# Layer 1 of a gated cross-attention kernel: one route for all probabilities, their low part on VectorE, the weights' rounding on ScalarE

## The chip, the cores and the metric

One core of one Trainium2 chip. The metric is the device time of one execution in microseconds (us). The kernel before takes 1699.95 us, the median of three executions (1699.6 to 1700.13).

## The reference, cut to what matters

Two layers run one after the other on x (8 x 128 x 512), each a gated cross-attention and a gated feed-forward block. The change lies in layer 1 and in the feed-forward block behind it:

```python
# layer 1: 32 query heads, 8 key/value heads, head size 128
z  = layernorm(x)
kv = concat([ctx, z], axis=1)               # 256 keys for each batch element
q  = rms_norm(z @ Wq, q_norm_w); k = rms_norm(kv @ Wk, k_norm_w); v = kv @ Wv
p  = softmax(q @ k.T / sqrt(128))           # 4 query heads share a key head
x  = x + tanh(g_xattn[1]) * ((p @ v) @ Wo)
x  = x + tanh(g_ffn[1]) * (layernorm(x) @ W_ffn.T + bias)
```

## The kernel before, in words

Matrix products run in three passes: each fp32 operand is split into a rounded high part (`_hi`) and the rest (`_lo`), and hi·hi, hi·lo and lo·hi are added up. So each operand needs a rounding (a copy) and a subtraction ahead of TensorE.

Layer 1 is cut into 64 items, one for a key/value head t (0 to 7) and a batch element j (0 to 7): `slot1(t, j)` is written once for every engine, and i = 8t + j is its number. A run of eight slots is called a turn below. The counts in the code start at 1, so `exponentials1(i)` works on the item before the one whose scores the slot makes. The slots of all engines are software-pipelined: slot i makes keys and values of item i+2, transposes queries and keys of item i+1, projects the output of item i-2, makes the queries of item i+2, the scores of item i+1 and the attention output of item i-1. Each engine works its list strictly in the written order; semaphores (`wait_ge`) are the only coupling.

The orders in a slot before the change:

- TensorE: `keys_values`, transposes of q, transposes of k, `output_projection1`, `queries`, scores, `attention_output1`.
- ScalarE: `exponentials1`, `qt_hi`, `kt_hi`, `moved_probabilities_hi` (L1246), `kv_out` (L1212, L1213), `q_out` (L1219), `output1_hi` (L1261).
- VectorE: `inverse_sums1` (L1964), `qt_lo` (L2004), `kt_lo` (L2006), `split_lo` (L1912), `accumulate1` (L1968), `probabilities_in_blocks` (L1983), `v_low` (L1922), `k_mean`, `split_hi` (L1906), `k_scaled` (L1929), `q_mean` (L1936), `maxima1` (L1954, with `nb` at L1959), `output1_lo` (L1992).
- GpSimd: `normalised` probabilities (L769), the probabilities' low part (L774), `k_root`, `q_root` (L631).

The probabilities p of an item must be transposed before they meet v. VectorE transposes them in 32 x 32 blocks, SyncE's queue writes the blocks to a DRAM buffer (L594) and, once that has landed, reads them back in the transposed order with four DMAs (L597). ScalarE then rounds them (`pt_hi`) and GpSimd makes the low part (`pt_lo`). The last four items do not take this route: TensorE transposes them into two PSUM banks (`transposed_probabilities1`, L2561), and ScalarE and VectorE split them from there; that also lets their output follow one slot earlier. `lagged(t, j)` says which route a slot takes.

The weights of the next head are loaded in five pieces of 128 x 1024 in a turn. VectorE rounds piece j in slot j (j below 5) and subtracts in slot j+1, so slots 1 to 5 of a turn have a subtraction and slots 0 to 4 a rounding. The last turn has neither.

PSUM has eight banks. The transposes of q and k go into the same banks as the products (`Q1B`, `KVB`), so `queries` waits until VectorE has read the transposed q (`qt_lo`), and banks 4 and 5 (`T0B`, `T1B`) are kept for the last four items.

After the last slot the feed-forward block of layer 1 runs by row tiles b (0 to 7): row statistics on VectorE, a root on GpSimd, `normed_rows` on VectorE, `transpose_rows(3, b)` on TensorE, `transposed_hi`/`transposed_lo`, `last_ffn(b)`, `feed_forward` and the store. Its steps stand between those of the last items, in an order written by hand.

## Time and profile before

| | |
|---|---|
| median of three executions | 1699.95 us |
| the profiled execution's own time | 1700.84 us |
| its span, first to last instruction | 1699.0 us |
| TensorE matmuls busy | 1651.3 us (97%) |
| VectorE busy | 1216.1 us (72%) |
| ScalarE busy | 987.6 us (58%) |
| GpSimd busy | 771.7 us (45%) |
| granted TensorE clock, mean | 0.999 of full speed |

Layer 1's slots fill about 943 to 1671 us of the span. In the 100 us from 1300 on, TensorE is shown busy 97.0%, VectorE 75.6%, ScalarE 58.6% and GpSimd 60.0%. Matmuls are pipelined, and each counts as busy until its modelled end, so that 97% is not TensorE at its peak: how long a slot takes is read better from the starts of one instruction in consecutive slots.

### The profile page before, as it was taken

The page shows a single profiled execution, that of the slowest core. Times are in us where ns is not written, and L with a number is a line of the kernel's source. Part 1 is how long each engine was busy: PE and PEld are TensorE (multiplying, and loading weights), DVE is VectorE, ACT ScalarE, POOL GpSimd, SP SyncE. Part 2 cuts the span into 40 slices and gives each one's busy share as a digit, 9 for nine tenths or more (in the row PEclk, how much of TensorE's full clock was granted, in tenths as well). Part 3 has the DMA queues.
Part 4 walks back from the last instruction along what each step waited for, and adds up shares of the span by engine and source line. Part 5 has one row for each costly group of instructions (what it writes and reads, how often), then busy time and mean ns, then how long its engine had stood idle before and what let it go on. Part 6 is the DMA issues. An engine that isn't in the chain of part 4 may idle for free.

```text
span 1699.0 us, 30580 instructions
## 1 busy us (share of the span) xinstructions
PE 1651.3 (97%) x9789; PEld 1426.0 (84%) x9789; DVE 1216.1 (72%) x2245; ACT 987.6 (58%) x2480; POOL 771.7 (45%) x644
## 2 busy tenths in 40 slices
PE   9999999999999999999999899999999999999998
PEld 8899999999988888888888777787878787777887
DVE  6444437676787777777788877777777777777777
ACT  5344343345767677676776566565656565665663
POOL 2422223211433443534435565566565656665554
PEclk9999999999999999999999999999999999999999
DMA  6444444545233333333332243434343444433311
GB/s 228 170 173 148 148 166 153 192 138 179 78 104 100 117 108 105 111 100 122 102 112 82 80 141 112 154 117 137 122 151 120 134 136 136 133 123 124 128 57 50
DMA packets 123792, 216.24 MB, mean 127 GB/s; under 512 B 11344, under 2 KB 93648, under 8 KB 120144
## 3 DMA queue, kind: packets, MB, share of 16 engines
q1 hardware_dynamic: 123728, 215.43, 38.0%
q8 instruction: 35, 0.57, 0.1%
q14 instruction: 29, 0.24, 0.0%
HBM read 139.89 MB, written 75.50 MB: 127 GB/s over the span
## 4 chain that ended last, share of the span: by engine, by line
PE 44%; DVE 28%; ACT 12%; issue 10%; POOL 4%; DMA 1%; DVEq 0%; SPq 0%; ACTq 0%; POOLq 0%
PE bank L2163 20%; ACT p L1237 7%; PE bank L2340 6%; DVE probabilities_in_blocks L1983 4%; PE bank L2110 4%; DVE v_lo L1922 3%; PE bank L2112 3%; PE bank L2111 3%; POOL k_r L631 3%; DVE nmax L1954 3%; DVE q_ss L1936 2%; PE bank L2298 2%; PE bank L2376 2%; DVE fbias L1929 2%; DVE qt_lo L2004 2%
## 5 line engine op out<-in xcount | busy, mean ns | idle before, releaser
L712 POOL TENSOR_TENSOR pr<-pr,rn 128x512 f32<-128x512 f32 x64 | 67.5, 1055 | 291.3 <-DVE rn L1610 291.3
L2110 PE MATMUL bank<-w_hi,xt_hi 128*128 (+2 forms) x512 | 182.5, 356 | 11.4 <-DVE qt_lo L2004 6.9
L769 POOL TENSOR_TENSOR p<-p,rn 128x512 f32<-128x512 f32 x128 | 133.2, 1041 | 128.3 <-DVE rn L1964 125.0
L1237 ACT ACTIVATE p<-bank,nb,q_r 128x256 f32<-128x256 f32 x256 | 141.2, 562 | 78.2 <-DVE nb L1959 78.1
L774 POOL TENSOR_TENSOR pt_lo<-probabilities_transposed,pt_hi 128x1024 fp32r<-128x1024 f32 x60 | 168.7, 2811 | 36.2 <-ACT pt_hi L1246 36.2
L2112 PE MATMUL bank<-w_hi,xt_lo 128*128 (+2 forms) x512 | 172.9, 338 | 0.0
L2111 PE MATMUL bank<-w_lo,xt_hi 128*128 (+2 forms) x512 | 172.2, 336 | 0.0
L2110 PEld LDWEIGHTS bank<-w_hi,xt_hi 128*128 128x128 f32 x512 | 96.3, 188 | 57.0 <-DVE qt_lo L2004 25.8
L2110 PE MATMUL bank<-w_hi,ot_hi 128*128 (+1 forms) x256 | 106.9, 418 | 18.3 <-DVE ot_lo L1992 16.1
L1079 ACT ACTIVATE pr<-sc,nmax 128x128 f32<-128x128 f32 x256 | 99.9, 391 | 39.8 <-DVE nmax L1595 39.4
L2110 PE MATMUL bank<-w0o_hi,ot_hi 128*128 128x512 f32 x256 | 105.4, 412 | 4.9 <-DVE residual L1602 4.4
L631 POOL TENSOR_TENSOR q_r<-q_ms,half 128x4 f32<-128x4 f32 x64 | 64.8, 1012 | 98.3 <-DVE q_ms L1938 98.3
L2112 PEld LDWEIGHTS bank<-w_hi,xt_lo 128*128 128x128 f32 x512 | 96.4, 188 | 11.1
L2163 PE MATMUL bank<-vw_hi,t_hi 128*128 128x256 f32 x368 | 104.1, 283 | 0.6 <-DVE vw_lo L1374 0.6
L2111 PEld LDWEIGHTS bank<-w_lo,xt_hi 128*128 128x128 f32 x512 | 96.7, 189 | 9.3
L2163 PE MATMUL bank<-vw_hi,t_lo 128*128 128x256 f32 x368 | 104.1, 283 | 0.0
L2163 PE MATMUL bank<-vw_lo,t_hi 128*128 128x256 f32 x368 | 104.1, 283 | 0.0
L2111 PE MATMUL bank<-w_lo,ot_hi 128*128 (+1 forms) x256 | 100.2, 391 | 0.0
L2112 PE MATMUL bank<-w_hi,ot_lo 128*128 (+1 forms) x256 | 100.2, 391 | 0.0
L2112 PE MATMUL bank<-w0o_hi,ot_lo 128*128 128x512 f32 x256 | 100.1, 391 | 0.0
L2111 PE MATMUL bank<-w0o_lo,ot_hi 128*128 128x512 f32 x256 | 100.0, 390 | 0.0
L1219 ACT ACTIVATE q_sb<-bank 128x512 f32<-128x512 f32 x64 | 38.3, 599 | 101.7 <-PE bank L2112 101.7
(298 smaller groups left out, 5517.8 us busy)
## 6 DMA issues: line engine op xcount, KB each, us to landing
blocks_of_probabilities<-probabilities_in_blocks SPq DMA_DIRECT2D x60, 512.0 KB, 2.9
probabilities_transposed<-blocks_of_probabilities SPq DMA_DIRECT2D x240, 128.0 KB, 2.8
stage<-w SPq DMA_DIRECT2D x35, 512.0 KB, 3.3
keys_of_layer<-kout SPq DMA_DIRECT2D x16, 1024.0 KB, 4.5
values_of_layer<-vout SPq DMA_DIRECT2D x16, 1024.0 KB, 5.2
kt<-keys_of_layer SPq DMA_DIRECT2D x64, 256.0 KB, 3.3
vs<-values_of_layer SPq DMA_DIRECT2D x64, 256.0 KB, 2.8
vraw<-wv SPq DMA_DIRECT2D x10, 1024.0 KB, 6.7
```

The source lines that it names most:

```text
L631: pool.tensor_tensor(dst, src, exponent, ALU.pow).then_inc(done, 1)
L712: pool.tensor_tensor(by4(pr), by4(pr), rn[:, :].unsqueeze(2).to_broadcast([P, 4, P]), ALU.mult).then_inc(norm_done, 1)
L769: pool.tensor_tensor(p1[:, half_p:half_p + 2, :], p1[:, half_p:half_p + 2, :], rn1[:, half_p:half_p + 2].unsqueeze(2).to_broadcast([P, 2, ...
L774: pool.tensor_tensor(pt_lo[:, :, :].rearrange("p kc (qb n) -> p kc qb n", qb=4), by_key_block(ptr1[:, (j - 1) % 2, :]), pt_hi[:, :, :].bit ...
L1079: last_op = nc.scalar.activation(by4(pr)[:, a, :], by4(sc)[:, a, :], ACT.Exp, bias=nmax[:, a:a + 1], accum_out=ssum[:, a:a + 1])
L1237: last_op = nc.scalar.activation(p1[:, a, :], by2((S0B, S1B)[a // 2][:, :])[:, a % 2, :], ACT.Exp, bias=nb1[:, a:a + 1], scale=q_r[:, pari ...
L1983: nc.vector.transpose(in_blocks(pblk[:, :])[:, half_p:half_p + 2], p1[:, half_p:half_p + 2, :].rearrange("p a (kc kb q) -> p a kc kb q", k ...
L2110: nc.tensor.matmul(out_ap, l_hi, r_hi, start=(c == 0), stop=False)
L2111: nc.tensor.matmul(out_ap, l_hi, r_lo, start=False, stop=False)
L2112: op = nc.tensor.matmul(out_ap, l_lo, r_hi, start=False, stop=(c == n - 1))
L2163: op = nc.tensor.matmul(out_ap, l, r, start=start, stop=False, skip_group_check=True)
L2340: op = nc.tensor.matmul(bank[which][:, :], l[:, a, c, :], r[:, c, :], start=start, stop=False, skip_group_check=True)
```

## The change

All 64 items take the DMA route, with the output one slot later; `transposed_probabilities1` and what belongs to it go. Banks 4 and 5 hold the transposed k and q (`KTB`, `QTB`), so `queries` and `keys_values` no longer wait for `qt_lo` and `kt_lo`. VectorE makes `pt_lo` instead of GpSimd. ScalarE rounds the weights instead of VectorE. `kv_out` leads the slot on ScalarE, `k_mean` on VectorE and `k_root` on GpSimd; `v_low` and `k_scaled` follow `kt_lo`. The order behind the last slot is written anew, with one more projection and one more attention output in it. In the first two slots of layer 1 four row tiles are transposed into banks 6 and 7 alone, and each waits for the one two before it.

```diff
-        KVB, Q1B, S0B, S1B, T0B, T1B, O1B, Y1B = bank
+        KVB, Q1B, S0B, S1B, KTB, QTB, O1B, Y1B = bank
-        XT_BANK = (..., (4, 5, 6, 7) * 2, (0, 0, 1, 0, 1, 0, 1, 0))
+        XT_BANK = (..., (4, 5, 6, 7, 6, 7, 6, 7), (0, 1) * 4)
# GpSimd, slot1
-                [normalised] [pt_lo] k_root(i + 2); q_root(i + 2, (j + 1) % 2)
+                k_root(i + 2); normalised(i); q_root(i + 2, (j + 1) % 2)
# ScalarE
+            def split_hi(n, piece, parity):
+                act.wait_ge(w1_in[piece], 16 * (n + 1))
+                cols = slice(1024 * piece, 1024 * (piece + 1))
+                nc.scalar.activation(w1_hi[:, parity, cols], stage1[:, piece % 2, :], ACT.Copy).then_inc(w1_hi_done[piece], 1)
             def slot1(t, j):
+                if not (last and j == BODY - 1):
+                    wait(act, o1_ps, i - 2)
+                    kv_out(i + 2, (j + 1) % 4, 4 * t + (j + 1) // 2 + 1)
                 if not (first and j == 0):
                     exponentials1(i, (j - 1) % 2)
...
+                if not (first and j < 2):
                     moved_probabilities_hi(i - 1, (j - 1) % 2)
-                if not (last and j == BODY - 1):
-                    wait(act, o1_ps, i - 2)
-                    kv_out(i + 2, (j + 1) % 4, 4 * t + (j + 1) // 2 + 1)
...
+                if not last and j < 5 and not (first and j == 0):
+                    wait(act, y1_ps if j >= 3 else q1_ps, 8 * t)
+                    split_hi(t + 1, j, (t + 1) % 2)
                 if not (last and j == BODY - 1):
                     q_out(i + 2)
# VectorE
+            def probabilities_lo(count, parity):
+                dve.wait_ge(pt1_hi_done, count)
+                nc.vector.tensor_tensor(pt_lo[:, :, :].rearrange("p kc (qb n) -> p kc qb n", qb=4), by_key_block(ptr1[:, parity, :]),
+                                        pt_hi[:, :, :].bitcast(fp32).rearrange("p kc (qb n) -> p kc qb n", qb=4),
+                                        ALU.subtract).then_inc(pt1_lo_done, 1)
             def slot1(t, j):
+                if ahead:
+                    k_mean(i + 2)
                 [inverse_sums1, qt_lo, kt_lo]
+                if ahead:
+                    v_low(i + 2, (j + 1) % 4)
+                    k_scaled(i + 2, (j + 1) % 4)
                 [split_lo, accumulate1]
+                if not (first and j < 2):
+                    probabilities_lo(i - 1, (j - 1) % 2)
                 [probabilities_in_blocks]
-                [v_low, k_mean, split_hi, k_scaled]
                 [q_mean, maxima1, output1_lo]
# TensorE, slot1
             def queries(b, parity, count):
-                wait(pe, qt1_lo_done, count - 1)
+                wait(pe, q1_copied, count - 1)
+                wait(pe, q1_squared, count - 1)
# TensorE, transpose_rows
-                        pe.wait_ge(xt_lo_done, count - 4)
+                        pe.wait_ge(xt_lo_done, count - (4 if phase_no == 1 else 2))
# TensorE behind the last slot (before: projection 63, rows 2 and 3, ffn 1, transposed
# probabilities 64, ffn 2, rows 4, attention 64, ffn 3, rows 5, projection 64, ...)
+            output_projection1(U - 2, last_own)
+            last_ffn(1)
+            transpose_rows(3, 2)
+            transpose_rows(3, 3)
+            attention_output1(U - 1, (BODY - 2) % 4)
+            last_ffn(2)
+            output_projection1(U - 1, last_own)
+            last_ffn(3)
+            transpose_rows(3, 4)
+            attention_output1(U, (BODY - 1) % 4)
+            last_ffn(4)
+            transpose_rows(3, 5)
+            output_projection1(U, last_own)
+            transpose_rows(3, 6)
+            last_ffn(5)
+            last_ffn(6)
+            transpose_rows(3, 7)
+            last_ffn(7)
```

Names in square brackets stand for calls that are there before and after. ScalarE's list behind the last slot is: exponentials 64, `transposed_hi` 1, `pt_hi` 63, `transposed_hi` 2 and 3, output 63, `transposed_hi` 4, `pt_hi` 64, output 64, `transposed_hi` 5 to 7. VectorE's has, among others: sums 64, blocks 64, accumulation of 62, row statistics, `transposed_lo` 2, `pt_lo` 63, output 63, accumulation of 63, row statistics, `transposed_lo` 4, `pt_lo` 64, output 64.

## Rows read from the trace of the kernel before

**Rows 1.** Waits from 1000 to 1600 us: engine, what waited, releaser, total us, times, longest.
```profile
PE bank L2110 <- DVE ot_lo L1992: 15.1, 33, 0.5
```
**Rows 2.** Timeline of a slot with weight work: start, us, engine, line, operation.
```profile
1341.22 0.56 ACT L1237 ACTIVATE p<-bank,nb,q_r 128x256 f32<-128x256 f32 x1 [1.73 <-DVE nb L1959]
...
1342.70 2.14 POOL L769 TENSOR_TENSOR p<-p,rn 128x512 f32<-128x512 f32 x2 [1.90 <-DVE rn L1964]
...
1345.04 1.22 DVE L1912 TENSOR_TENSOR w_lo<-stage,w_hi 128x1024 f32 x1
...
1346.83 1.30 DVE L1983 STREAM_TRANSPOSE probabilities_in_blocks<-p 128x512 f32<-128x512 f32 x2
...
1348.05 0.63 DVE L1922 TENSOR_TENSOR v_lo<-keys_values_of_context,v_hi 128x128 fp32r<-128x128 f32 x1
...
1348.87 0.68 DVE L1906 TENSOR_SCALAR w_hi<-stage 128x1024 f32 x1
...
1350.13 0.29 DVE L1929 TENSOR_SCALAR fbias<-keys_values_of_context,k_r 128x128 f32<-128x128 f32 x1 [0.59 <-POOL k_r L631]
...
1350.60 0.68 DVE L1936 TENSOR_REDUCE q_ss<-q_sq 128x4 f32<-128x512 f32 x1
...
1352.99 0.56 ACT L1237 ACTIVATE p<-bank,nb,q_r 128x256 f32<-128x256 f32 x1 [1.70 <-DVE nb L1959]
```
**Rows 3.** Timeline: nb starts the exponentials; slot 0 of turns 1 and 7, next slot.
```profile
1044.57 0.16 DVE L1959 TENSOR_TENSOR nb<-nmax,q_r 128x4 f32<-128x4 f32 x1
...
1590.07 0.17 DVE L1959 TENSOR_TENSOR nb<-nmax,q_r 128x4 f32<-128x4 f32 x1
...
1600.67 0.17 DVE L1959 TENSOR_TENSOR nb<-nmax,q_r 128x4 f32<-128x4 f32 x1
```
**Rows 4.** One line from 960 us on: count, duration ns min/median/max.
```profile
L1922 DVE TENSOR_TENSOR v_lo<-keys_values_of_context,v_hi x61: 279/628/1696, 970.7 to 1654.0; 128x128 fp32r<-128x128 f32 x61
```
**Rows 5.** Timeline of the DMA route: a late one up to pt_hi; an undisturbed store.
```profile
1006.52 0.33 SPq L594 DMA_DIRECT2D blocks_of_probabilities<-probabilities_in_blocks  x1
...
1011.04 1.75 SPq L597 DMA_DIRECT2D probabilities_transposed<-blocks_of_probabilities  x4
...
1015.56 1.06 ACT L1246 ACTIVATE pt_hi<-probabilities_transposed 128x1024 fp32r<-128x1024 f32 x1 [1.52 <-DMA probabilities_transposed<-blocks_of_probabilities]
...
1574.87 0.34 SPq L594 DMA_DIRECT2D blocks_of_probabilities<-probabilities_in_blocks  x1
...
1577.53 1.74 SPq L597 DMA_DIRECT2D probabilities_transposed<-blocks_of_probabilities  x4
```
**Rows 6.** Timeline: attention output, keys and values, q transposes, and ScalarE behind them.
```profile
1303.87 0.40 PE L2110 MATMUL bank<-pt_hi,v_hi 128*128 128x512 f32 x1
...
1305.26 0.28 PE L2110 MATMUL bank<-w_hi,xt_hi 128*128 x1
...
1305.46 0.60 ACT L1261 ACTIVATE ot_hi<-bank 128x512 fp32r<-128x512 f32 x1 [1.73 <-PE bank L2112]
...
1306.68 0.60 PE L2587 MATMUL bank<-ident,q_sb 128*128 128x128 f32 x4
...
1311.06 0.30 ACT L1212 ACTIVATE v_hi<-bank 128x128 fp32r<-128x128 f32 x1
...
1311.38 0.24 ACT L1213 ACTIVATION_READ_ACCUMULATOR fbias<-bank 128x1 f32 x1
```
**Rows 7.** Timeline of TensorE: the queries of layer 1's third slot.
```profile
968.09 0.51 PE L2110 MATMUL bank<-w_hi,xt_hi 128*128 128x512 f32 x1 [3.49 <-DVE qt_lo L2004]
```
**Rows 8.** Timeline behind the last turn: exponentials of item 63, the last accumulation.
```profile
1661.31 0.56 ACT L1237 ACTIVATE p<-bank,nb,q_r 128x256 f32<-128x256 f32 x1 [0.46 <-DVE nb L1959]
...
1695.72 0.75 DVE L1799 SCALAR_TENSOR_TENSOR residual<-bank,tg,residual 128x512 f32<-128x512 f32 x1 [1.09 <-PE bank L2460]
```
**Rows 9.** Chain that ended last: start, us; a feed-forward tile, a row tile's transposes.
```profile
1682.43 1.84 PE bank L2460 x8
1684.26 0.44 PE bank L2132 x4
```

More of the change, by code:

```diff
@@ L1231, in exponentials1 @@
                 act.wait_ge(shift1_done, count)
-                if isinstance(count, int) and count > LAGGED + 1:
-                    act.wait_ge(pt1_ps, count - 1 - LAGGED)
-                else:
-                    wait(act, blocks1_done, 2 * (count - 1))
+                wait(act, blocks1_done, 2 * (count - 1))
                 for a in range(4):
@@ L1247, in moved_probabilities_hi @@
                                      ACT.Copy).then_inc(pt1_hi_done, 1)
-            def probabilities_hi(count):
-                act.wait_ge(pt1_ps, count - LAGGED)
-                wait(act, o1_ps, count - 1)
-                for kc in range(2):
-                    nc.scalar.activation(pt_hi[:, kc, :], (T0B, T1B)[kc][:, :], ACT.Copy).then_inc(pt1_hi_done, 1)
             def output1_hi(count):
@@ L1293, in slot1 @@
                     transposed_hi(2, 5)
-                if (lagged(t, j) or i == LAGGED + 1) and not (first and j < 2):
+                    split_hi(1, 0, 1)
+                if not (first and j < 2):
                     output1_hi(i - 1)
-                if not lagged(t, j):
-                    if i == LAGGED + 1:
-                        probabilities_hi(i)
-                    output1_hi(i)
                 if last and 3 <= j < 3 + C:
@@ L2026, in slot1 @@
                     nc.vector.tensor_scalar(fbias1, fbias16, tg[:, 3:4], None, ALU.mult)
-                if ahead:
-                    v_low(i + 2, (j + 1) % 4)
-                    k_mean(i + 2)
-                if last and j in (5, 6):
-                    normed_rows(3, 2 * j - 10)
-                    normed_rows(3, 2 * j - 9)
+                if last and j in (5, 7):
+                    normed_rows(3, j - 5)
+                    normed_rows(3, j - 4)
+                if last and j == BODY - 1:
+                    transposed_lo(3, 0)
                 if first and j == 0:
@@ L2038, in slot1 @@
                     transposed_lo(2, 7)
-                if not last and j < 5 and not (first and j == 0):
-                    wait(dve, y1_ps if j >= 3 else q1_ps, 8 * t)
-                    split_hi(t + 1, j, (t + 1) % 2)
-                if not lagged(t, j) and LAGGED + 1 < i < U - 1:
-                    probabilities_lo(i)
                 if ahead:
-                    k_scaled(i + 2, (j + 1) % 4)
                     q_mean(i + 2)
-                if i == LAGGED + 1 if isinstance(i, int) else False:
-                    output1_lo(i - 1)
-                    probabilities_lo(i)
                 maxima1(i + 1, j % 2)
-                if last and i == LAGGED + 1:
-                    accumulate1(i - 1, (j - 2) % B)
-                    dve.wait_ge(acc1_done, i - 1)
-                    row_stats(3, 1)
                 if first and j == 0:
@@ L2058, in slot1 @@
                     transposed_lo(2, 5)
-                    split_hi(1, 0, 1)
-                if lagged(t, j) and not (first and j < 2):
+                if not (first and j < 2):
                     output1_lo(i - 1)
-                if not lagged(t, j):
-                    output1_lo(i)
             for j in range(BODY):
@@ L2595, in slot1 @@
                     pe.wait_ge(first_lo, 5)
-                if (lagged(t, j) or i == LAGGED + 1) and not (first and j < 3):
+                if not (first and j < 3):
                     output_projection1(i - 2, own if j >= 3 else other)
@@ L2612, in slot1 @@
                     pe.wait_ge(facc_done, B)
-                if not lagged(t, j) and i == LAGGED + 1:
-                    attention_output1(i - 1, (j - 2) % 4)
                 pe.wait_ge(qt1_lo_done, i + 1)
@@ L2621, in slot1 @@
                 op.then_inc(s1_ps, 1)
-                if lagged(t, j) and not (first and j < 2):
+                if not (first and j < 2):
                     if first and j == 2:
```

193 lines of the change are left out of this document (73 added, 120 removed).

## The prediction

> **What bounds the kernel now.** I read the table of the page first: TensorE is busy 97% and nothing else above 72%, which looks as if only less TensorE work could help. The waits say nearly the same: from 1000 to 1600 us TensorE is shown idle only 15.1 us, for VectorE's `ot_lo` [rows 1]. The starts of one instruction in consecutive slots correct this. Six turns (48 slots) take 1590.07 - 1044.57 = 545.5 us, 90.92 a turn or 11.36 a slot, but a slot without weight work takes 10.60 [rows 3]. A slot with it takes 1352.99 - 1341.22 = 11.77 from one first exponential to the next [rows 2]. So in the slots with weight work TensorE is not the limit; its pipelined matmuls hide the missing time in their spans. What closes the 11.77 us is a ring: `nb` releases the exponentials on ScalarE, these `qt_hi`, and from there VectorE works through its list (rows at 1345.04 to 1350.60, each start on the end of the one before) up to the next `nb`. The one gap in it, 0.59 us, is `k_scaled` waiting for GpSimd's `k_r`. VectorE's average of 72% hides this too: it stands still only while the exponentials run.
>
> **The change part by part.**
>
> *The ring in slots with weight work.* Out of it go: the rounding `w_hi` and the wait for `k_r`, 1350.13 - 1348.87 = 1.26 us [rows 2]; `k_mean`, 0.07, now beside the exponentials; and the excess of `v_low`. Its SBUF half takes 0.63 us in this slot and at the median, 0.28 at the least [rows 2, 4]; GpSimd is making `pt_lo` at that moment. With `pt_lo` gone from GpSimd I take 0.28, a gain of 0.35; if it met GpSimd's `normalised` instead, it could gain nothing or lose 1 us (the 1.70 at the longest). `normalised` ends 3.62 us after the first exponential (1342.70 + 2.14 - 1341.22) and `v_low` would begin at 3.82 (1345.04 - 1341.22), so they just miss [rows 2]. Into it comes `pt_lo`. VectorE never did it before; the nearest row is `w_lo`, same form and size, 1.22 us [rows 2], of which 0.09 lies beside the next instruction: 1.13. Were the strided operand half as fast it would be 2.2; nothing suggests less than 1.1. Sum: 11.77 - 1.26 - 0.07 - 0.35 + 1.13 = 11.22.
>
> The Trainium skill, "SBUF — State Buffer", section "Who interferes with whom", has a rule for the 0.63: a VectorE instruction with two SBUF inputs and a GpSimd instruction that reads SBUF exclude each other. The rows agree (0.28 alone, up to 1.70), and by that rule `pt_lo`, with two such inputs, would be blocked itself if it met `normalised`; on this schedule it begins 6.5 us after the first exponential and does not.
>
> *The rounding on ScalarE* costs what `pt_hi` of the same size costs, 1.06 us [rows 5]. It stands ahead of `q_out`, where ScalarE (58.6% busy) waits for the queries' product anyway, so it lies in idle time. Without that cover `q_out` and then `q_mean` would be late by at most the 1.06.
>
> The Trainium skill, "ScalarE: Activation LUTs", section "Rules for kernel authors", would have simple arithmetic stay on VectorE. The rows agree on the single instruction (0.68 against 1.06). Kept there, 0.60 would stay in the ring (11.82, no gain); the idle engine decides here, not the faster one.
>
> *`kv_out` ahead of the exponentials* adds a wait: all of ScalarE's list queues behind the keys-and-values product. `pt_lo` ends 7.72 after the first exponential (3.82 + 0.42 `v_low` + 0.47 `k_scaled` + 1.79 `split_lo` and `accumulate1` = 6.50, + 1.22). Attention output and keys and values follow in 1306.68 - 1303.87 = 2.81, plus 0.1 for a start after a wait; ScalarE answers 0.20 later (1305.46 against 1305.26); the second half of `kv_out` takes 0.32 and about 0.1 of its reading before the exponential can start [rows 6]. With 0.05 to release TensorE that is 11.30, against 11.22 for the first ring. So 11.3 decides, in slots 1 to 5.
>
> *The DMA route* now closes a ring of its own, as `pt_lo` (behind `pt_hi`) and the next item's blocks stand in one list. Store to loads 2.66, loads to `pt_hi` 4.52 at the one place where ScalarE waited for it, `pt_hi` 1.06, releases 0.1 [rows 5], `pt_lo` 1.13, blocks 1.30: 10.77. The loads of that place followed a slow store, so I take 4.4 and 10.65. In slots without weight work the first ring is only 11.22 - 1.13 = 10.1, so there the route decides: 10.65 instead of 10.60 to 10.7, no gain. Slot 6 lies between 10.65 and 11.3, as TensorE comes late out of slot 5; I take 11.0. A turn: 5 x 11.3 + 11.0 + 2 x 10.65 = 88.8, against 90.92: -2.1, and -12.7 in six turns.
>
> *The first turn.* `queries` no longer waits for `qt_lo` (idle 3.49 in the third slot [rows 7]). Against that, row tile 4 must wait in slot 0 until VectorE has done tile 2, behind `k_scaled`; I see the queries of slot 0 start about 3.4 us later (two `transposed_lo` and a chain through `k_root` ahead of them). The next two slots win that back. I take 0, bounds -4 and +4.
>
> *The last turn, up to the exponentials of item 63.* Before: 1661.31 - 1590.07 = 71.24 [rows 3, 8]. After: six slots of 10.65 and about 3.5 us of row statistics and `normed_rows` on VectorE that lengthen them (six passes of 128x512 at about 0.6, half of `w_lo`), 0.3 to the exponential: 67.7, or -3.5. Before, the move to TensorE's transposes made these slots longer.
>
> *Behind it.* Before, 1661.31 to the end of the span at 1699.0: 37.7. After, counted from that exponential: item 63's blocks end at 6.9, and item 64's at 15.05, since its exponentials start only at 10. VectorE takes up `pt_lo` of 63 at 17.9, behind an accumulation and row statistics: TensorE waits 2.5 us for it, until 19.15. Then attention 63 (1.45), ffn 2 (1.85 [rows 9]), projection 63 (2.85: 12 matmuls of 0.23 and a start), ffn 3 (1.85), row tile 4 (0.44 [rows 9]): 27.6. Item 64 came back from DRAM at 22, but ScalarE's `pt_hi` stands behind `transposed_hi` of tile 4: 0.8 for that, 1.06 and 1.22 for the parts, so TensorE stands again, until 30.7. Attention 64, ffn 4, tile 5, projection 64, tile 6, ffn 5, 0.45 of waiting, ffn 6, tile 7: 11.65, so 42.35. High and low part of tile 7 1.55, ffn 7 1.85, accumulation 0.95, store 1699.0 - 1695.72 - 0.75 = 2.53 [rows 8]: 49.25, and 0.65 for what GpSimd's additions will slow on VectorE: 49.9. That is +12.2, bounds +8 (the row work moves less) and +15.
>
> *Sum* against the profiled execution (1700.84, of which 1699.0 span): 0 - 12.7 - 3.5 + 12.2 = -4.0. It ran 0.9 above the median 1699.95; the same difference from the median gives 1696.0.
>
> **Rivals.**
>
> *The round trip decides everywhere (slower).* VectorE's whole list now queues behind `pt_lo`, thus behind DRAM. Before, a late `pt_hi` held only GpSimd. For it: once the route took 9.04 from store to `pt_hi` (1006.52 to 1015.56) [rows 5]. Against: the weight load now starts 2.9 us ahead of the store instead of 1.7. It decides from 0.2 us above my 7.1 on; at 7.55 some 27 slots gain 0.4 to 0.45 each, +11: 1707.
>
> *The wait ahead of the exponentials eats the gain (even).* If `kv_out` comes 0.15 later than worked out, by an uncounted start in TensorE's list, the 35 slots of 11.3 become 11.45 to 11.5: +5: 1701.
>
> *A cheaper end (faster).* If VectorE gets to both `pt_lo` 2 us earlier each and slots 1 to 5 stay at the first ring (11.2), it is 1696 - 4 - 3.5: 1688.
>
> **How the numbers follow.** Forecast (1691 to 1699.5) 0.45, round trip 0.20, even 0.23, cheaper end 0.12. The range 1685 to 1708 takes in the bounds of the turn, the first turn and the end. Faster by over 0.2% (below 1696.55; less than that cannot be told from no change) is 0.33 of the forecast, all of the cheaper end and 0.01 of the even case: 0.46. Slower (above 1703.35): the round trip and 0.05 of the even case: 0.25. Within: 0.29.
>
> **What would show it.** Exponential to exponential 11.3 in slots 1 to 5 and 10.65 in 6, 7 and 0; `k_scaled` no longer waiting for `k_r`; `v_lo` at 0.28; `pt_hi` waiting for the DMA in nearly every slot by about 1.5 us; TensorE no longer waiting for `qt_lo`; behind the last slot two TensorE waits of 2.5 and 3.1 us, and 50 us from the exponentials of 63 to the end. A `pt_lo` well above 1.22, a `pt_lo` that waits in slots 1 to 5, or exponentials released by `kv_out` instead of `nb` there would make it wrong on the slow side; a slot of 11.0 or less on the fast side.

## The result, and the profile after

The changed kernel takes 1706.24 us (median of 9 runs) beside 1699.95 us for the kernel before in the same runs; the ratio is 1.0033, 95% interval 1.0022 to 1.0044. One of these executions (1790.74 us, granted clock 0.846) and one of a later run (2689.81 us, 0.556) were slow, and the ratios leave them out. So the change makes the kernel slower by about a third of a per cent, where 1696.0 was forecast. The time lies inside the range of 1685 to 1708, but on the other side of the kernel before than the forecast.

The profiled execution took 1706.54 us with a span of 1704.7, that is 5.7 more than the span before (1699.0). Four stretches, cut at the same instructions in both traces, add up to it:

```
stretch                                        before    after    change  forecast
layer 1, first turn (and what leads to it)    1044.57  1049.96     +5.4       0
six turns in the loop                          545.50   533.13    -12.4     -12.7
last turn, to the exponentials of item 63       71.24    69.53     -1.7      -3.5
from there to the end of the span               37.69    52.08    +14.4     +12.2
sum                                                                +5.7      -4.0
```

The loop did what was forecast. Timeline of the changed kernel in a slot with weight work (start, us, engine, line, operation):

```profile
1351.13 0.57 ACT L1235 ACTIVATE p<-bank,nb,q_r 128x256 f32<-128x256 f32 x1
...
1355.35 0.28 DVE L1913 TENSOR_SCALAR fbias<-keys_values_of_context,k_r 128x128 f32<-128x128 f32 x1
...
1357.60 1.21 DVE L1957 TENSOR_TENSOR pt_lo<-probabilities_transposed,pt_hi 128x1024 fp32r<-128x1024 f32 x1
...
1362.03 0.16 DVE L1943 TENSOR_TENSOR nb<-nmax,q_r 128x4 f32<-128x4 f32 x1
...
1362.41 0.57 ACT L1235 ACTIVATE p<-bank,nb,q_r 128x256 f32<-128x256 f32 x1
```

From exponential to exponential it is 11.28 us; before it was 11.77 [rows 2]. `k_scaled` (L1913) no longer waits for `k_r`, and `pt_lo` takes 1.21 us. The exponentials start 0.22 us after `nb` has ended: `kv_out` ahead of them holds them up, not `nb`, as the sum had it (11.30 for that ring, 11.22 for VectorE's list). The other parts of the loop answer to the forecast too. In the groups of instructions, `pt_hi` waits for the DMA 1.48 us on average (94.6 / 64), and `v_lo`, 628 ns at the median before [rows 4], is at 281 everywhere:

```profile
L1244 ACT ACTIVATE pt_hi<-probabilities_transposed 128x1024 fp32r<-128x1024 f32 x64 | 68.0, 1063 | 94.6 <-DMA probabilities_transposed<-blocks_of_probabilities 94.6
L1906 DVE TENSOR_TENSOR v_lo<-keys_values_of_context,v_hi x62: 278/281/285, 962.7 to 1644.8; 128x128 fp32r<-128x128 f32 x62
```

The loss stands outside the loop. TensorE in the first turn of the changed kernel, with VectorE's first `nb`:

```profile
944.09 0.60 PE L2547 MATMUL bank<-ident,q_sb 128*128 128x128 f32 x4
949.00 1.94 PE L2103 MATMUL bank<-ident,z_mid 128*128 128x128 f32 x8 [4.10 <-DVE xt_lo L1349]
950.60 0.78 PE L2079 MATMUL bank<-w_hi,xt_hi 128*128 128x512 f32 x1
954.93 0.28 PE L2079 MATMUL bank<-kt_hi,qt_hi 128*128 128x256 f32 x1
958.37 0.16 DVE L1943 TENSOR_TENSOR nb<-nmax,q_r 128x4 f32<-128x4 f32 x1
973.43 0.36 PE L2079 MATMUL bank<-kt_hi,qt_hi 128*128 128x256 f32 x1 [3.94 <-DVE kt_lo L1987]
976.59 0.77 PE L2079 MATMUL bank<-pt_hi,v_hi 128*128 128x512 f32 x1 [0.97 <-DVE pt_lo L1957]
979.29 0.41 PE L2079 MATMUL bank<-w_hi,xt_hi 128*128 128x256 f32 x1
```

The same two places before, the query transposes of slot 0 and the first `nb`:

```profile
944.18 0.60 PE L2587 MATMUL bank<-ident,q_sb 128*128 128x128 f32 x4
952.94 0.16 DVE L1959 TENSOR_TENSOR nb<-nmax,q_r 128x4 f32<-128x4 f32 x1
```

Both kernels reach slot 0 at the same time; then it takes 14.28 us to the first bias of the exponentials instead of 8.76. The wait of 4.10 us is the one forecast (row tile 4 behind tile 2). But the queries behind it take 4.33 us (950.60 to 954.93) instead of the 2.87 that they took before (946.63 to 949.50). The windows of the changed kernel say why; their columns are, behind the stretch and its length, busy time and count of PE, PEld, DVE, ACT and POOL, then TensorE's granted clock, DMA share and GB/s:

```profile
948.00:952.00 4.00, 3.00 (x11) 2.76 (x12) 1.46 (x4) 0.47 (x1) 0.00 (x0) 0.50 0.11 33
952.00:956.00 4.00, 4.00 (x19) 3.37 (x18) 0.00 (x0) 0.87 (x2) 0.00 (x0) 0.77 0.00 0
...
972.00:976.00 4.00, 2.20 (x12) 1.93 (x12) 3.76 (x8) 2.68 (x5) 1.04 (x1) 0.79 0.32 79
976.00:980.00 4.00, 3.41 (x10) 2.86 (x11) 3.76 (x8) 1.34 (x3) 1.01 (x1) 0.50 0.75 262
...
1652.00:1656.00 4.00, 2.75 (x7) 2.21 (x8) 2.05 (x6) 3.38 (x11) 4.00 (x5) 0.69 0.44 131
1656.00:1660.00 4.00, 3.88 (x23) 3.22 (x23) 2.63 (x5) 1.33 (x2) 1.45 (x2) 0.88 0.00 0
...
1672.00:1676.00 4.00, 2.90 (x9) 2.28 (x10) 2.38 (x4) 0.60 (x1) 0.10 (x1) 0.75 0.80 243
1676.00:1680.00 4.00, 4.00 (x16) 3.25 (x15) 2.27 (x4) 0.00 (x0) 2.78 (x2) 0.82 0.09 36
```

A clock of 0.50 is the lower of its two levels, 1.2 instead of 2.4 GHz. It was granted behind TensorE's wait of 4.10 us, again behind the 3.94 us of slot 2, and twice in the end, behind the waits ahead of these starts:

```profile
1653.25 0.55 PE L2079 MATMUL bank<-w_hi,ot_hi 128*128 128x512 f32 x1 [2.66 <-DVE ot_lo L1971]
1657.69 0.60 PE L2103 MATMUL bank<-ident,plain 128*128 128x128 f32 x4
1673.10 0.50 PE L2079 MATMUL bank<-pt_hi,v_hi 128*128 128x512 f32 x1 [2.39 <-DVE pt_lo L1957]
1683.70 1.05 ACT L1244 ACTIVATE pt_hi<-probabilities_transposed 128x1024 fp32r<-128x1024 f32 x1
1686.07 0.50 PE L2079 MATMUL bank<-pt_hi,v_hi 128*128 128x512 f32 x1 [2.89 <-DVE pt_lo L1957]
```

From 1648 to 1660 the kernel before held 1.00. The waits of 2.39 and 2.89 us are the two that were forecast (2.5 and 3.1).

### The profile page after: what moved, and what is told of

It reads as the page before. It is cut to its first block, busy times and chain, and to the rows that moved or that the text cites. A ratio compares the mean times of both kernels' runs of the same rounds, so it can differ in the third digit from the quotient of the medians.

```text
span 1704.7 us, 30549 instructions
## 1 busy us (share of the span) xinstructions
PE 1643.4 (96%) x9757; PEld 1436.2 (84%) x9757; DVE 1230.3 (72%) x2274; ACT 1022.6 (60%) x2511; POOL 589.8 (35%) x584
## 4 chain that ended last, share of the span: by engine, by line
PE 58%; DVE 20%; ACT 9%; DMA 6%; issue 5%; SPq 1%; POOL 1%; DVEq 0%; ACTq 0%; POOLq 0%
PE bank L2134 20%; PE bank L2079 8%; PE bank L2080 8%; PE bank L2081 8%; PE bank L2311 6%; ACT p L1235 4%; DMA probabilities_transposed<-blocks_of_probabilities 2%; DMA blocks_of_probabilities<-probabilities_in_blocks 2%; DVE pt_lo L1957 2%; PE bank L2269 2%; PE bank L2347 2%; DVE probabilities_in_blocks L1966 2%; PE bank L2431 2%; DVE w_lo L1896 2%; DVE wl L1575 1%
## 5 line engine op out<-in xcount | busy, mean ns | idle before, releaser
L2079 PE MATMUL bank<-w_hi,xt_hi 128*128 (+2 forms) x512 | 173.4, 339 | 0.1
L1244 ACT ACTIVATE pt_hi<-probabilities_transposed 128x1024 fp32r<-128x1024 f32 x64 | 68.0, 1063 | 94.6 <-DMA probabilities_transposed<-blocks_of_probabilities 94.6
L1250 ACT ACTIVATE ot_hi<-bank 128x512 fp32r<-128x512 f32 x64 | 38.3, 598 | 119.2 <-PE bank L2081 119.2
L2079 PEld LDWEIGHTS bank<-w_hi,xt_hi 128*128 128x128 f32 x512 | 97.0, 189 | 13.9 <-POOL w_lo L728 0.3
L2081 PEld LDWEIGHTS bank<-w_hi,xt_lo 128*128 128x128 f32 x512 | 96.8, 189 | 10.9
L1948 DVE RECIPROCAL rn<-sum 128x2 f32<-128x2 f32 x128 | 21.2, 166 | 110.9 <-ACT p L1235 110.9
```

The costliest lines, as they stand in the source:

```text
L1244: nc.scalar.activation(pt_hi[:, :, :].rearrange("p kc (qb n) -> p kc qb n", qb=4), by_key_block(ptr1[:, parity, :]), ACT.Copy).then_inc(pt ...
L1250: nc.scalar.activation(by_head(ot1_hi[:, :]), by_query_block(O1B[:, :]), ACT.Copy).then_inc(ot1_hi_done, 1)
L2079: nc.tensor.matmul(out_ap, l_hi, r_hi, start=(c == 0), stop=False)
L2081: op = nc.tensor.matmul(out_ap, l_lo, r_hi, start=False, stop=(c == n - 1))
```

## The experiments

Theory A: the loop gained what was forecast; the hand-written orders of the first turn and of the end lose it, partly by TensorE's waits and partly by the half clock behind them. Rival B: these waits lie beside the ring of the items, which sets the time anyway. The last runs take the loop's own terms apart. All ratios are to the kernel before in the same runs, and "profiled" stretches are cut as in the table above.

**Queries ahead of the row tiles (first turn).**

```
                 output_projection1(i - 2, ...)
+            if ahead:
+                queries(...)
             if first and j < 2:
                 transpose_rows(2, 4 + 2 * j)
                 transpose_rows(2, 5 + 2 * j)
-            if ahead:
-                queries(...)
```

> The changed kernel with one edit: in slots 0 and 1 of the first turn TensorE issues the queries ahead of the two transposes of row tiles, instead of behind them. Theory A (the order by hand in the first turn costs the head): TensorE's wait of 4.10 us at 949.00 for row tile 2's low part then no longer stands ahead of the queries of item 2, the first bias of the exponentials comes about 5 us earlier (958.4 to about 953.5), and about 4 of the 5.4 us lost in the first turn come back: total near 1702, 4 us below the changed kernel's 1706.2. Rival B (the ring of an item is full in the first turn anyway, so what is won at slot 0 is lost in the waits of slots 2 to 4, where TensorE waits 3.9 us for kt_lo and the loads take 4.8 us): the first bias comes earlier, but turn 1 begins within 1 us of where it began (1049.96): total 1705.5 to 1706.5.

Measured: 1698.99 us, ratio 0.9990 (0.9981 to 0.9999), 7.3 us below the changed kernel by the two ratios. Its trace:

```profile
944.51 0.60 PE L2547 MATMUL bank<-ident,q_sb 128*128 128x128 f32 x4
945.08 0.48 PE L2079 MATMUL bank<-w_hi,xt_hi 128*128 128x512 f32 x1
949.47 1.23 PE L2103 MATMUL bank<-ident,z_mid 128*128 128x128 f32 x8 [1.34 <-DVE xt_lo L1349]
953.50 0.16 DVE L1943 TENSOR_TENSOR nb<-nmax,q_r 128x4 f32<-128x4 f32 x1
1041.69 0.17 DVE L1943 TENSOR_TENSOR nb<-nmax,q_r 128x4 f32<-128x4 f32 x1
```

From the query transposes to the first bias it is 8.99 us (14.28 without the edit, 8.76 before), and turn 1 begins 97.2 us after them (1041.69 - 944.51), against 105.9 in the changed kernel and 100.4 before. Theory A holds and the gain is larger than expected: with this order the first turn is 3.2 us shorter than before. The forecast expected some gain here from `queries` no longer waiting for `qt_lo`; how much of the 3.2 us that is was not taken apart.

**Matmuls in TensorE's waits, first turn.**

```
+            if first and j == 0:            # ahead of the transposes of row tile 4
+                pe.wait_ge(facc_done, 7)
+                warm(S0B, 15)
...
+            if first and j == 2:            # ahead of the scores
+                pe.wait_ge(xt_lo_done, 3 * B)
+                warm(O1B, 14)
```

`warm(bank, n)` issues n matmuls of 128x512.

> The changed kernel with matmuls added whose results are overwritten: 15 of 512 columns ahead of the transposes of row tile 4 (slot 0) and 14 ahead of the scores of slot 2, both in first turn, where TensorE waited 4.1 and 3.9 us; nothing else moves. Theory A (a part of the head's loss is the granted clock, which fell to 0.50 behind these waits): queries of slot 0 take about 2.85 us instead of 4.33, attention of slot 2 1.4 instead of 2.7, keys and values 1.4 instead of 2.2; turn 1 begins 2 to 4 us earlier, total 1702.5 to 1704. Rival B (the waits alone made the loss, the clock ran beside the exponentials and the DMA round trip): the clock stays at 1.0 but turn 1 begins within 1 us of 1049.96, total 1705.5 to 1706.5. A loss (1707 or more) would say that the added matmuls themselves delay the work behind them.

Measured: 1704.61 us, ratio 1.0023 (1.0015 to 1.0032). The clock is 1.00 in all of the windows from 940 to 984; the queries of slot 0 take 2.85 us; the first bias comes 12.23 us after the query transposes instead of 14.28; slot 2 lasts 11.40 us from bias to bias instead of 13.40; turn 1 begins 101.3 us after the query transposes, against 105.9 in the changed kernel and 100.4 before. A holds for the first turn, while the total lies just above its range: by the ratio it gains 1.7 us, too little to tell from nothing with these intervals. Its profile shows where the rest went: the six turns take 535.4 us instead of 533.1, with three loads that follow their store by 3.9 to 4.4 us, and in the end the clock falls behind the wait of 2.89 us (0.59 from 1684 to 1688).

**Matmuls in TensorE's waits, last turn and end.**

```
+            if last and j == BODY - 1:      # ahead of the projection of item 61
+                pe.wait_ge(acc1_done, i - 3)
+                warm(Y1B, 9)
...
+        pe.wait_ge(ot1_lo_done, U - 2)      # ahead of the attention of item 63
+        warm(O1B, 8)
```

> The changed kernel with matmuls added whose results are overwritten: 9 of 512 columns ahead of the projection of item 61 (slot 63, where TensorE waited 2.66 us) and 8 ahead of the attention of item 63 (where it waited 2.39 us). Theory A (the end is 2 us longer than forecast because the granted clock falls behind these waits): the clock stays near 1.0 from 1652 to 1680, projection 61 takes about 2.85 us instead of 4.44, attention 63 about 1.4 instead of 1.96 and the next feed-forward 1.85 instead of 2.95; total 1703 to 1704.5. Rival B (the stretches at half clock ran beside the round trip of item 63 and the exponentials and cost nothing): the clock stays near 1.0 and the total is 1705.5 to 1706.5.

Measured: 1704.32 us, ratio 1.0022 (1.0011 to 1.0033). The windows that stood at 0.69, 0.88, 0.75 and 0.82 are now at 1.00, the one behind them is not:

```profile
1652.00:1656.00 4.00, 4.00 (x26) 3.45 (x24) 2.66 (x5) 3.24 (x8) 3.36 (x4) 1.00 0.24 72
1656.00:1660.00 4.00, 2.55 (x11) 1.68 (x11) 4.00 (x8) 0.60 (x1) 0.00 (x0) 1.00 0.32 131
1672.00:1676.00 4.00, 4.00 (x19) 3.33 (x18) 2.26 (x4) 0.09 (x1) 2.65 (x2) 1.00 0.38 144
1676.00:1680.00 4.00, 2.29 (x13) 1.68 (x11) 2.57 (x6) 1.54 (x2) 0.69 (x2) 1.00 0.00 0
1680.00:1684.00 4.00, 2.82 (x7) 2.26 (x8) 1.79 (x2) 0.00 (x0) 0.00 (x0) 0.58 0.19 66
```

TensorE at the wait ahead of the attention of item 64 in this run:

```profile
1681.18 0.80 PE L2079 MATMUL bank<-pt_hi,v_hi 128*128 128x512 f32 x1 [2.89 <-DVE pt_lo L1957]
```

The slot up to item 64's bias shortens from 11.28 to 10.05 us, which lies behind the exponentials of item 63, and that whole stretch from 52.08 to 50.6. But the clock now falls at the next wait, as the last window shows: behind the wait of 2.89 us, where the changed kernel kept 1.00, it is 0.58, and the attention of item 64 takes 2.73 us instead of 1.49. Up to the start of that attention the stretch is 2.8 us shorter (30.64 us, against 33.45). Again the interval overlaps that of the changed kernel, so the clock needed a run with all four.

**All four, beside the changed kernel itself.**

> The changed kernel, its orders untouched, with all four groups of added matmuls (results overwritten): 15 and 14 of 512 columns in the first turn, 9 and 8 in the last turn and the end. Theory A (the half clock behind TensorE's waits costs time on the path in head and end): the two single runs' gains of about 1.7 and 1.9 us by ratio add, total about 3 to 4 us below the changed kernel run beside it. Rival B (the single runs' differences were scatter): within 1 us of the changed kernel run beside it.

> The changed kernel itself, as the measure for the run with all four groups of added matmuls, on the same chip: 1704 to 1707 (ratio to the kernel before 1.0022 to 1.0044). In its trace the slot of the first turn in which the clock falls (slot 2) is compared with the first profile: if the clock is at 0.5 in it while the scores, the attention and the keys and values run, the next slot starts 13.4 us later as there; if it is back before the attention, 11.4 us (Theory A). Rival B: 13.4 us whatever the clock is.

Measured on the same chip: 1700.82 us, ratio 1.0003 (0.9994 to 1.0012), with the matmuls; 1703.97, ratio 1.0025 (1.0015 to 1.0035), without. The intervals don't meet: 3.2 us between the medians, where A expected 3 to 4 and B less than 1. So adding work, with nothing moved, takes away 3.2 of the 3.8 us by which the changed kernel was slower than the one before in these runs: that much is the clock's, with one fall of it still in the run. In the profile with the matmuls the clock is 1.00 from 940 to 1676; turn 1 begins 101.0 us after the query transposes, 3.2 earlier than without. Behind the last wait it falls (0.74, 0.50 and 0.91 from 1676 to 1688), so the end takes 52.1 us as without the matmuls:

```profile
1678.53 0.80 PE L2079 MATMUL bank<-pt_hi,v_hi 128*128 128x512 f32 x1 [2.89 <-DVE pt_lo L1957]
```

This attention of item 64 starts 2.8 us earlier in the end (30.61 us against 33.42), and the half clock behind it takes the 2.8 back. Two late stores (4.97 and 4.76 us to their loads) lengthen the last turn of this profile by 2.4, so the two profiled spans differ by only 1.4 us; the 3.2 rest on the medians. In the second profile of the changed kernel the clock was 0.50 in 976 to 980 as in the first, and slot 2 lasted 13.44 us, as expected there. Its other stretches show what else varies from run to run:

```
stretch (us)                            after   again
query transposes of slot 0 to turn 1    105.9   104.2
six turns                               533.1   533.1
last turn, to the exponentials of 63     69.5    68.1
from there to the end                    52.1    52.1
```

The difference is in the first and the last turn. SyncE's queue of the first profile shows one cause, the second profile at the same item the undisturbed case:

```profile
991.09 0.33 SPq L592 DMA_DIRECT2D blocks_of_probabilities<-probabilities_in_blocks  x1
995.86 1.75 SPq L595 DMA_DIRECT2D probabilities_transposed<-blocks_of_probabilities  x4
```

```profile
991.25 0.33 SPq L592 DMA_DIRECT2D blocks_of_probabilities<-probabilities_in_blocks  x1
993.91 1.75 SPq L595 DMA_DIRECT2D probabilities_transposed<-blocks_of_probabilities  x4
```

The loads follow their store by 4.77 us instead of 2.66. In the first profile this happens twice in 64 items (here, slot of 12.86 us against 11.22, and at 1581.11, slot of 12.45 against 10.85), in the second not at all (3.46 us at the longest).

**The end in another order.**

```
 ScalarE:  output1_hi(U - 1)
-          transposed_hi(3, 4)
           moved_probabilities_hi(U, U % 2)
           output1_hi(U)
+          transposed_hi(3, 4)
 VectorE:  feed_forward(3, last_gate, 2)
+          probabilities_lo(U, U % 2)
           accumulate1(U - 1, 6)
...
 TensorE:  output_projection1(U - 1, last_own)
-          last_ffn(3)
+          attention_output1(U, (BODY - 1) % 4)
           transpose_rows(3, 4)
-          attention_output1(U, (BODY - 1) % 4)
+          last_ffn(3)
...
```

> The changed kernel with the order of its end rewritten, no instruction added or taken out: ScalarE rounds the probabilities of item 64 (moved_probabilities_hi) ahead of row tile 4 of the last phase, VectorE takes their low part ahead of the accumulation of item 63 and the rows behind it, and TensorE does the attention of item 64 right behind the projection of item 63, the feed-forward of row tile 3 behind it. Theory A (the end is longer than forecast because its hand-written order puts item 64 behind row tiles): the rounding of item 64 starts when its loads land, about 1676.6 instead of 1683.7, the end from the exponentials of item 63 shrinks from 52.1 us to about 45, total near 1699. Rival B (the end is set by the row tiles' own chain, feed-forward after feed-forward, and by the half clock behind TensorE's waits, not by the place of item 64): total 1704.5 to 1706.5.

Measured: 1696.41 us, ratio 0.9981 (0.9972 to 0.9989), 8.8 us below the changed kernel by the ratios. The rounding of item 64 now waits for its loads and for nothing else, and the attention behind it does not wait at all:

```profile
1671.04 1.06 ACT L1244 ACTIVATE pt_hi<-probabilities_transposed 128x1024 fp32r<-128x1024 f32 x1 [0.24 <-DMA probabilities_transposed<-blocks_of_probabilities]
1676.02 0.44 PE L2078 MATMUL bank<-pt_hi,v_hi 128*128 128x512 f32 x1
```

The rounding starts 23.2 us after the exponentials of item 63 (at 1647.87 here), against 31.1 (1683.70 - 1652.62) in the changed kernel, and the end takes 46.8 us instead of 52.1; A expected about 45. The other 3.5 us of the total are in the first and last turn, which this edit doesn't touch and in which the two profiles of the changed kernel differ by 3.2 as well; about 5 us are the order's. A part of that scatter is the clock: in slot 2 of the first turn it was back at 0.90 from 976 to 980 here, and the slot took 11.46 us instead of 13.40.

**Both orders.** The two edits in one kernel.

> The changed kernel with both reorderings together: queries ahead of the row tiles' transposes in slots 0 and 1 of the first turn, and item 64 ahead of row tiles in the end. Theory A (head and end are separate losses of the two hand-written orders): their gains add, 7.3 + 8.8 us from the ratios of the single runs, total near 1690, ratio to the kernel before about 0.994. Rival B (a part of what the single runs gained was an earlier phase of the ring that both share): less than 13 us together, total 1693 or more.

Measured: 1691.81 us, ratio 0.9957 (0.9944 to 0.9971). By the ratios 12.9 us of the expected 16 came, which is B's number. The stretches of the profile don't bear B out: the first turn keeps its gain (96.8 us from the query transposes to turn 1) and so does the end (45.2), and the profiled spans add (1704.7 to 1696.6 and to 1694.7 alone, to 1686.8 together). But the profiled execution was the fastest of the five (1688.64 to 1693.7), so it can't settle why the median falls short of the sum, and that stays open.

**Row statistics behind the bias.**

```
-            if last and j in (4, 6):
-                dve.wait_ge(acc1_done, i - 2)
-                row_stats(3, (4, 6).index(j))
...
             output1_lo(i - 1)
+            if last and j in (4, 6):
+                dve.wait_ge(acc1_done, i - 2)
+                row_stats(3, (4, 6).index(j))
```

> As the run with both reorderings, and in the last turn VectorE takes the row statistics of slots 4 and 6 behind the bias and the low part of the output, at the end of the slot, instead of ahead of them; GpSimd adds the bias to the first two row tiles one slot later. Theory A (the last turn gained 1.7 us instead of 3.5 because 1.6 us of row statistics stand ahead of nb and ot_lo in these slots, and TensorE's waits of 1.7 and 2.7 us for ot_lo are theirs): slots 4 and 6 shorten from 12.4 and 11.9 to about 10.7 each, the fall of the clock in the last slot goes, 3 to 5 us below the run with both. Rival B (the statistics only move, and hold up the next slot's k_mean and the end instead): within 1 us of the run with both.

Measured: 1690.02 us, ratio 0.9951 (0.9937 to 0.9965). Rival B for the most part: slot 4 of the last turn shortens from 12.40 to 10.79 us, and slot 6 from 11.92 to 9.96, but slot 5 grows from 10.87 to 12.20, as the statistics now run while VectorE would take up the next item. The last turn wins 2.1 us and the end gives 1.5 of them back (46.7 us instead of 45.2). By the ratios this kernel is 14 us below the changed one; against the run before it the difference can't be told from nothing.

**The same with matmuls in the two waits that are left.**

> The run with both reorderings and the late row statistics, with matmuls added whose results are overwritten: 14 of 512 columns ahead of the scores of slot 2 of the first turn, 8 ahead of the attention of item 63. Theory A (the half clock that is left behind TensorE's waits of 3.9 us in the first turn and 2.4 us in the end costs time on the path): clock 1.0 there, 1.5 to 3 us below the run without them (1690), ratio to the kernel before 0.9935 to 0.9945. Rival B (with the orders mended, what is left of half clock lies beside the exponentials and the DMA round trip): the clock is 1.0 and the total within 1 us of 1690.

Measured: 1691.24 us, ratio 0.9944 (0.9930 to 0.9958). The clock is 1.00 throughout, but the intervals are nearly the same, so whether the half clock still costs anything stays open. Its profile has five items whose loads follow the store by 4.25 to 4.73 us, where the run without the matmuls has none, and that hides a difference of this size.

**The loop's terms, one by one.** Three runs undo one part of the change each.

The rounding of the weights back on VectorE, ahead of `q_ss`:

```
 ScalarE: -   wait(act, ...); split_hi(t + 1, j, (t + 1) % 2)
 VectorE: +   wait(dve, ...); split_hi(t + 1, j, (t + 1) % 2)
              q_mean(i + 2)
```

> The changed kernel with the weights' rounding put back on VectorE, ahead of q_ss as in the kernel before; all else as in the changed kernel. Theory A (the prediction's statement that the rounding kept on VectorE would leave 0.60 us in the ring): the bias nb comes 0.6 us later in slots 1 to 5, the exponentials are released by it and no longer by kv_out, these slots take 11.75 us instead of 11.27, 35 slots give 17 us: total 1720 to 1726. Rival B (kv_out behind the attention decides and VectorE has 0.5 us to spare in these slots): slots stay within 0.1 of 11.27, total 1705 to 1710.

Measured: 1715.88 us, ratio 1.0097 (1.0082 to 1.0112). Timeline:

```profile
1334.86 0.16 DVE L1944 TENSOR_TENSOR nb<-nmax,q_r 128x4 f32<-128x4 f32 x1
1343.95 0.65 DVE L1891 TENSOR_SCALAR w_hi<-stage 128x1024 f32 x1
1346.63 0.16 DVE L1944 TENSOR_TENSOR nb<-nmax,q_r 128x4 f32<-128x4 f32 x1
```

A slot takes 11.77 us, as A had it (11.75), and six turns 545.8: what they took before (545.50). The first turn and the last lose nothing by it (91.3 and 68.6 us where the changed kernel takes 91.6 and 69.5), and the end takes 50.8 us instead of 52.1, hence 11 us by the ratios and not 17. The end is shorter because the clock stayed at 1.00 behind the wait ahead of projection 61 (2.65 us here), with no matmuls added.

The probabilities' low part back on GpSimd:

```
 VectorE: -   probabilities_lo(i - 1, (j - 1) % 2)
 GpSimd:      normalised(i)
          +   pool.tensor_tensor(pt_lo, ptr1, pt_hi, ALU.subtract)
              q_root(i + 2, (j + 1) % 2)
```

> The changed kernel with the probabilities' low part put back on GpSimd, where it took about 2.9 us in the kernel before, between the normalising and the query root; all else as in the changed kernel. Theory A (the prediction's second ring: attention, keys and values and with them kv_out and the exponentials queue behind the low part): the low part ends about 8.7 us after the first exponential instead of 7.7, the slots with weight work go from 11.27 to about 12.2 us and the others follow the same chain, 11.5 or more; total 1745 to 1775. Rival B (VectorE's list closes the ring, and taking 1.13 us from it shortens it as the sum with 1.13 for the low part says): slots with weight work 10.7 or less, total below 1690.

Measured: 1760.04 us, ratio 1.0354 (1.0336 to 1.0372): A's size, by A's mechanism and a second one that A did not have. Timeline:

```profile
1343.86 0.50 PE L2082 MATMUL bank<-pt_hi,v_hi 128*128 128x512 f32 x1 [0.29 <-POOL pt_lo L779]
...
1345.42 0.16 DVE L1948 TENSOR_TENSOR nb<-nmax,q_r 128x4 f32<-128x4 f32 x1
...
1347.40 0.57 ACT L1240 ACTIVATE p<-bank,nb,q_r 128x256 f32<-128x256 f32 x1
...
1351.58 2.41 POOL L779 TENSOR_TENSOR pt_lo<-probabilities_transposed,pt_hi 128x1024 fp32r<-128x1024 f32 x1 [0.56 <-ACT pt_hi L1249]
1351.62 2.44 DVE L1918 TENSOR_SCALAR fbias<-keys_values_of_context,k_r 128x128 f32<-128x128 f32 x1
1359.34 0.16 DVE L1948 TENSOR_TENSOR nb<-nmax,q_r 128x4 f32<-128x4 f32 x1
```

`k_scaled`'s half from SBUF takes 2.44 us instead of 0.28, for just as long as GpSimd is at `pt_lo`, and everything behind it on VectorE up to `nb` is 2.2 us late. That is the second mechanism. A's is there too: the attention waited for the low part, and with `kv_out` behind it the exponentials start 1.98 us after the start of the bias, where the changed kernel has 0.3 to 0.4 in most slots with weight work. Together they make 13.92 us between two biases. Slots of 12.2 to 13.9 us come in about every other place (the ones between take 10.1 to 11.5). The Trainium skill, "SBUF — State Buffer", section "Who interferes with whom", names `tensor_scalar` among the VectorE operations that can take the port pair shared with GpSimd, and says that the second one then fully blocks; the rows of `pt_lo` and `k_scaled` agree.

The key chain back behind the exponentials:

```
 ScalarE: -   kv_out(...)            # ahead of exponentials1
              moved_probabilities_hi(...)
          +   kv_out(...)
 VectorE: -   k_mean; v_low; k_scaled      # first half of the slot
              probabilities_in_blocks(i)
          +   v_low; k_mean; ...; k_scaled; q_mean
```

> The changed kernel with the key chain back in the second half of the slot: kv_out behind pt_hi on ScalarE, v_lo and k_mean behind the blocks on VectorE, k_scaled ahead of q_mean, the key root behind the normalising on GpSimd; the rest of the change stays (pt_lo on VectorE, the rounding on ScalarE, the end by DMA). Theory A (the forecast's ring, in which VectorE's wait of 0.59 us for k_r and 0.07 us of k_mean come back): slots with weight work 11.27 to about 11.9 us, slots without it 10.5 to about 10.8; 35 and 29 slots give 20 to 30 us, total 1725 to 1735. Rival B (the wait of the exponentials for kv_out, which goes here, costs as much as the wait for k_r that it replaced): slots with weight work within 0.2 of 11.27, total 1703 to 1712.

Measured: 1736.18 us, ratio 1.0209 (1.0193 to 1.0225). Timeline:

```profile
1340.05 0.16 DVE L1942 TENSOR_TENSOR nb<-nmax,q_r 128x4 f32<-128x4 f32 x1
1349.63 0.29 DVE L1912 TENSOR_SCALAR fbias<-keys_values_of_context,k_r 128x128 f32<-128x128 f32 x1 [0.81 <-POOL k_r L630]
1352.20 0.16 DVE L1942 TENSOR_TENSOR nb<-nmax,q_r 128x4 f32<-128x4 f32 x1
```

The wait for `k_r` is back with 0.81 us and the slot takes 12.15, which is 11.27 with the 0.81 and 0.07 for `k_mean`; slots without weight work take 11.02. A holds, with the wait longer than the 0.59 of before [rows 2], and the total 1 us above its range.

## Why the prediction was wrong

*The six turns: right.* -12.4 against -12.7, with slots of 11.27 for the 11.3 forecast. What decides is what the sum said: `kv_out` behind the attention holds up the exponentials, by 0.22 us, with VectorE's list right behind it. Putting parts of that list back shows its worth: 0.65 us of rounding in it is worth all that the turns gained (545.8 us with it back), and the late key chain brings its wait for `k_r` back with 0.81. That ScalarE hides the rounding is shown as well. The prediction's list of signs contradicts its sum in one place: exponentials released by `kv_out` were to make it wrong, though by the sum they had to be. One detail was off: the slot that follows slot 0 takes about 11.7 us, and the slots without weight work about 10.6; the two cancel.

*The first turn: the step that failed.* The prediction saw the queries of slot 0 start about 3.4 us later and went on: "The next two slots win that back. I take 0." The delay by the order alone was 3.5 us: 12.23 us with the clock held up, less the 8.76 of before. What the 0 left out is the half clock behind the waits. With the clock held by matmuls, turn 1 begins 101.3 and 101.0 us after the query transposes (two runs), against 100.4 before: all of the 3.5 but 0.6 to 0.9 is won back, 1.8 of it in slots 0 and 1 (10.86 and 10.43 us, where before they took 11.39 and 11.68). Without them the queries behind the first wait ran at half clock (2.1 us to the first bias, 14.28 - 12.23), and in slot 2 TensorE waited again, fell to half clock and made it 13.40 (11.40 with the clock held). In this profile slot 3 also met a store of 4.77 us (12.86 against 11.22). +5.4, outside the bound of 4 that the prediction gave; by the second profile, from the query transposes on, it is +3.8 (104.2 - 100.4).

*The last turn: -1.7 against -3.5.* The second profile gives -3.2, so most of this miss is the late store of the first (12.45 against 10.85 us for its slot). The row statistics were in the sum.

*The end: +14.4 against +12.2, the same in both profiles.* The sum's order of events was right, to the two waits and to the rounding of item 64 queued behind row tile 4. What it left out is again the half clock, and one wait that is none of its terms: the 2.66 us for `ot_lo` at 1653.25. Behind it the exponentials of item 64 start 11.28 us after those of item 63, where the sum had 10; with the clock at 1.00 they start at 10.0 (with the matmuls, and without any in the run with the rounding back on VectorE). Behind the next wait attention 63 and the feed-forward take 4.9 us (1673.10 to 1678.01) for the 3.3 of the sum. So the attention of item 64 starts at 33.45 us instead of 30.7. With the clock held behind both waits it starts at 30.64 and 30.61: there the sum was right to 0.1. The rest took 18.6 us at full clock (52.08 - 33.45) for 19.2 in the sum, which is the sum without its 0.65 for GpSimd's additions; the trace does not show that term.

*The rivals.* "The round trip decides everywhere" gave 1707 and came nearest in time, but not for its reason: the six turns took what was forecast, and the late stores are a few items. Two of the three rivals were mechanisms of the loop and the third a cheaper end; none asked what a wait does to TensorE's clock, though the prediction itself listed TensorE waits of 2.5 and 3.1 us in the end and 3.4 us at the head. By the run with all four groups of matmuls that is 3.2 us, with a fall behind the last wait still in it.

## What to carry to other kernels

A steady loop can be forecast from one ring; a first and a last turn whose order is written by hand need the same care, since what they lose comes out of the loop's gain (here 12.4 us won in six turns, 18 lost outside them). Where a change makes TensorE wait for microseconds, price the work behind the wait at half clock too, and look first for independent work to put in front of the wait: one swap of two calls in the first turn was worth 7 us, a new order of the end about 5, while with matmuls put into the first two waits of the end the clock fell behind the third. With both orders, the change is faster than the kernel before: 1690 to 1692 us.

## What the runs showed of the hardware

In the changed kernel the clock fell behind waits of TensorE of 4.10, 3.94, 2.66 and 2.39 us, but not behind the one of 2.89 us at 1686.07 (1.00 from 1680 to the end). In the kernel before it fell behind a wait of 2.65 us (0.57 from 956 to 960), but not behind the one of 3.49 us at 968.09 (1.00 from 968 to 976). The same wait can go either way: the one ahead of projection 61 (2.66 us, and 2.65 there) left it at 1.00 in the run with the rounding back on VectorE, and the one of 2.89 us brought 0.58 and 0.50 in the runs whose added matmuls had filled the two waits ahead of it, and 0.64 in the run with the queries ahead of the row tiles, which has none. So the length of one wait does not by itself tell whether the clock falls.

The store of the probabilities, from issue to the issue of its loads, takes 2.68 us at the median in most of the profiles (2.92 in the kernel before, 2.94 with the low part on GpSimd); in places it takes 4.2 to 5.0. That was so for 2 of 64 items in the first profile of the changed kernel, 0 in the second, 3 with all four groups of matmuls, 5 and 0 in the fastest order with and without matmuls, all of them in the first two turns or from 1573 us on. With all items on the DMA route such a store lengthened the slot by 1.6 us in both cases of the first profile (12.86 against 11.22, 12.45 against 10.85). The three profiles with matmuls added in the first turn have 3, 3 and 5 such stores, all others with every item on the DMA route 0 to 2, so a part of what the matmuls win may be lost to them. What makes them late was not tried.
